# Zero rows of the routed buffers written inside the attention's loop, and Wg turned in other PSUM banks

## The reference

```python
x = x + xattn(layernorm(x), ctx)        # ctx: 32 x 1601 x 512
x = x + attn(layernorm(x))              # "attn": a recurrence over the 64 steps
x = x + ffn(layernorm(x))               # 8 experts, 2 of them per token

# xattn: softmax over the context, feats = [h, hq, h*hq, h*hc] @ W_qv + b_qv
# attn:
z = sigmoid(x @ Wg.T + bg)
h = df * h + (1 - df) * (z_t * (x_t - (h @ Wr.T + br)))     # df = sigmoid(decay)
y = (layernorm(h) * ln_w + ln_b) @ Wo.T + bo
# ffn: top 2 of softmax(x @ gate_w.T), weights normed, then per expert
out = (silu(x @ gate) * (x @ up)) @ down
```

## Time and profile before

| | |
|---|---|
| median of 3 runs | 1304.49 us (1302.57 to 1305.15) |
| the profiled execution | 1303.37 us |
| its span, first to last instruction | 1301.6 us |
| mean granted TensorE clock | 0.969 of full speed |
| PE, DVE, ACT, POOL busy | 1204.4, 724.4, 451.6, 591.9 us |
| moved by DMA | 225.22 MB, mean 173 GB/s |

### The profile page before, as it was taken

The page is one execution under the profiler, slowest core; times in us unless marked ns, Lnnn a source line. Parts: engine busy times, 40 slices in busy tenths (PEclk is TensorE's granted clock), DMA queues, the critical chain, the costliest instruction groups (busy, mean ns, idle before and its releaser), DMA issues. The chain is left out here.

```text
span 1301.6 us, 29765 instructions
## 1 busy us (share of the span) xinstructions
PE 1204.4 (93%) x10484; PEld 742.4 (57%) x10485; DVE 724.4 (56%) x1508; ACT 451.6 (35%) x1006; POOL 591.9 (45%) x641
## 2 busy tenths in 40 slices
PE   2899999999999999999989699997699999999993
PEld 1344444444444344444367477775588888888882
DVE  5555566655557665555379667787632323223235
ACT  3443445443445544344156243543111111212110
POOL 1123333222333321333069567887296564531972
PEclk9899999999999999999989799997799999999997
DMA  9644565444566444466074678752114344412556
GB/s 332 240 166 163 212 218 207 142 170 152 200 218 218 171 158 159 173 212 211 10 235 138 220 246 292 258 185 109 50 58 165 139 161 145 161 56 72 154 162 186
DMA packets 95187, 225.22 MB, mean 173 GB/s; under 512 B 10088, under 2 KB 26600, under 8 KB 91024
## 3 DMA queue, kind: packets, MB, share of 16 engines
q1 hardware_dynamic: 78912, 181.05, 40.3%
q0 software_dynamic: 10288, 33.57, 7.6%
q10 hardware_dynamic: 5920, 9.72, 2.3%
HBM read 178.95 MB, written 45.35 MB: 172 GB/s over the span
## 5 line engine op out<-in xcount | busy, mean ns | idle before, releaser
L323 POOL TENSOR_TENSOR wb<-wb,w 128x512 f32<-128x512 f32 x120 | 149.4, 1277 | 338.3 <-ACT wb L509 338.3
L393 PE MATMUL S<-ctxT,x 32*64 32x416 f32 (+1 forms) x4096 | 184.9, 508 | 13.9 <-DVE ctxT L649 13.3
L393 PEld LDWEIGHTS S<-ctxT,x 32*64 32x64 f32 x4096 | 109.3, 132 | 90.8 <-issue 44.8
L631 DVE STREAM_TRANSPOSE ctxT<-ctx_one 128x1024 f32<-128x1024 f32 (+1 forms) x128 | 115.0, 947 | 24.6 <-DMA ctx_one<-in_ctx_dram 24.5
L428 PE MATMUL O<-ctx_one,probsT 128*64 128x512 f32 (+1 forms) x448 | 110.7, 609 | 0.0
L523 ACT ACTIVATE x<-S,w2R,w3R 128x128 f32<-128x128 f32 x256 | 93.6, 492 | 19.2 <-PE S L384 19.2
L2048 POOL TENSOR_TENSOR w_low<-w_low,w_high 128x2048 fp32r<-128x2048 f32 x21 | 96.8, 4609 | 1.7
L2226 DVE TENSOR_TENSOR f_hL<-f_TH,f_hH 128x512 fp32r<-128x512 f32 x39 | 27.0, 692 | 116.9 <-ACT f_hH L2186 116.9
L2191 ACT ACTIVATE sg<-f_G 128x512 f32<-128x512 f32 x39 | 23.4, 599 | 193.7 <-PE f_G L2133 193.7
L1511 PE MATMUL Pb<-w_high 128*32 128x128 f32 x2016 | 70.7, 283 | 10.3 <-DVE w_high L1802 10.2
L509 ACT ACTIVATE wb<-w,hcb 128x512 f32<-128x512 f32 x120 | 77.6, 746 | 0.0
(11 more groups left out here) (298 smaller groups left out, 2491.5 us busy)
## 6 DMA issues: line engine op xcount, KB each, us to landing
ctx_one<-in_ctx_dram SPq DMA_DIRECT2D x64, 512.0 KB, 4.5
x<-in_ctx_dram SPq DMA_DIRECT2D x16, 1536.0 KB, 9.5
ctx_two<-in_ctx_dram SPq DMA_DIRECT2D x16, 1536.0 KB
ctx_one<-in_ctx_dram SPq DMA_DIRECT2D x64, 256.0 KB, 5.4
w_low<-_L_ffn_gate_up_proj_dram POOLq DMA_DIRECT2D x10, 1024.0 KB, 7.7
f_xt<-routed_x SPq DMA_DIRECT2D x39, 256.0 KB, 2.7
routed_y<-f_yt SPq DMA_DIRECT2D x39, 256.0 KB, 2.0
w_low<-_L_ffn_gate_up_proj_dram SPq DMA_DIRECT2D x6, 1024.0 KB, 12.8
```

Source lines behind the costliest of these rows:

```text
L323: pool.tensor_tensor(wb[:, slot, b], wb[:, slot, b], w0[:, c], ALU.add).then_inc(wb_ready, 1)
L393: last = pe.matmul(S[64 * b:64 * b + 64, a, 0:tiles * Q], qr[a * Q:(a + 1) * Q, k, 64 * b:64 * b + 64], ctxT[a * Q:(a + 1) * Q, 0:tiles, b ...
L631: return dve.transpose(ctxT[:, pos:pos + n, b], src[:, i:i + n, :].rearrange("p t (k r) -> p t k r", r=Q))
```

## The change

Two edits that have nothing to do with each other.

*The zeros.* The buffers `routed_x` and `routed_y` are declared in a new class `RoutedRows` ahead of the attention, which gets it as `rows`. POOL clears a tile `zero` of 128x128 at the attention's start. SP writes 24 tiles of `routed_y`, two at the end of each body of the loop, and behind the last step, ahead of `ahead.load`, the 8 pads and 7 spare tiles of `routed_x`. Each write is 256 KB as before, but its source is the 128x128 tile taken four times, so its runs are 128 floats instead of 512. `routed_y` gets one tile more (24 in place of 23). In the recurrence the writes, their waits and the `memset` go; `load_ahead` keeps the experts' weights.

*Wg.* TensorE turns Wg into the banks `WR` instead of `g_T` and `g_Z`. Its wait for all four `wgL` moves from ahead of `turn(0, 0)` to ahead of `gates(0, 0)`. On DVE `low_x(0, 0)` moves ahead of `statistics(2, 0)`.

```diff
+            def zeros(out):
+                sp.dma_start(out, zero[:, None, :].to_broadcast([P, C, P])).then_inc(zero_out, 16)
...
+            assert rows.UNWRITTEN == 2 * (PAIRS - 4)
             step(0, 0, True, False)
+            sp.wait_ge(zero_set, 1)
             with sp.Fori(0, (PAIRS - 4) // 2) as i:
                 step(2 * i + 1, 1, True, True)
+                zeros(rows.unwritten[sp.snap(4 * i)])
+                zeros(rows.unwritten[sp.snap(4 * i + 1)])
                 step(2 * i + 2, 0, True, True)
+                zeros(rows.unwritten[sp.snap(4 * i + 2)])
+                zeros(rows.unwritten[sp.snap(4 * i + 3)])
             step(PAIRS - 3, 1, True, True)
             step(PAIRS - 2, 0, False, True)
+            for e in range(sh.E):
+                zeros(rows.pads[e])
+            for n in range(rows.spare):
+                zeros(rows.spares[n])
...
+            sp.wait_ge(zero_out, 16 * (rows.UNWRITTEN + sh.E + rows.spare))
...
                 pool.wait_ge(tail_zero, b + 1)
+            pool.memset(zero[:], 0.0).then_inc(zero_set, 1)
             pool.memset(mhalf[:], -0.5).then_inc(consts, 1)
...
-        WT = T + Z
         WR = [stack.enter_context(nc.psum_tensor(f"g_W{n}", [P, 512], F32)) for n in range(C)]
...
             pe.wait_ge(ahead.w_in, 16)
             for k in range(C):
                 for c in range(C):
-                    last = pe.transpose(WT[k][:, c * P:(c + 1) * P], wg_rows[:, k, c * P:(c + 1) * P], ident[:])
+                    last = pe.transpose(WR[k][:, c * P:(c + 1) * P], wg_rows[:, k, c * P:(c + 1) * P], ident[:])
                 last.then_inc(wT_full, 1)
-            pe.wait_ge(wL_ready, C)
...
             turn(0, 0)
             turn(1, 1)
+            pe.wait_ge(wL_ready, C)
             gates(0, 0)
...
-                act.copy(wgH[:, :, k * P:(k + 1) * P], WT[k][:].rearrange("p (c e) -> p c e", c=C)).then_inc(wH_ready, 1)
+                act.copy(wgH[:, :, k * P:(k + 1) * P], WR[k][:].rearrange("p (c e) -> p c e", c=C)).then_inc(wH_ready, 1)
...
-                dve.tensor_tensor(wgL[:, :, part], WT[k][:].rearrange("p (c e) -> p c e", c=C), wgH[:, :, part].bitcast(F32),
+                dve.tensor_tensor(wgL[:, :, part], WR[k][:].rearrange("p (c e) -> p c e", c=C), wgH[:, :, part].bitcast(F32),
...
             for k in range(C):
                 low_w(k)
+            low_x(0, 0)
             statistics(2, 0)
-            low_x(0, 0)
...
+class RoutedRows:
+
+    UNWRITTEN = 24
+
+    def __init__(self, nc, sh):
         self.region = P + sh.N
         self.tiles = (2 * sh.N + sh.E * (P - 1)) // P
         self.spare = self.tiles - 2 * sh.N // P
         self.rows = sh.E * self.region + self.spare * P
+        self.x_rows = nc.dram_tensor("routed_x", (self.rows, sh.D), F32, kind="Internal").ap()
+        self.y_rows = nc.dram_tensor("routed_y", (self.tiles * P, sh.D), F32, kind="Internal").ap()
+        regions = self.x_rows[0:sh.E * self.region, :].rearrange("(e r) d -> e r d", e=sh.E)
+        self.pads = regions[:, 0:P, :].rearrange("e p (s i) -> e p s i", i=P)
+        self.spares = self.x_rows[sh.E * self.region:, :].rearrange("(n p) (s i) -> n p s i", p=P, i=P)
+        last = self.y_rows[(self.tiles - self.UNWRITTEN) * P:, :]
+        self.unwritten = last.rearrange("(n p) (s i) -> n p s i", p=P, i=P)
+        assert self.tiles - self.UNWRITTEN <= sh.N // P
...
-        zero, xn3T = ex.rows(1, 2)[0:2]
+        xn3T = ex.rows(1, 2)[1]
...
-            pads = [e * rt.region for e in range(E)] + [E * rt.region + i * P for i in range(rt.spare)]
-
-
-
-            AHEAD = TILES - 2
-            first_unwritten = sh.N // P
-            unwritten = [range(first_unwritten + i, rt.tiles, AHEAD) for i in range(AHEAD)]
-
             def load_ahead(k):
 
-                if k == 0:
-                    sp.wait_ge(zero_set, 1)
-                else:
+                if 0 < k <= ex.SLOTS * ex.PARTS:
                     sp.wait_ge(h_ready, ST * k)
-                for r in pads[k::AHEAD]:
-                    sp.dma_start(rt.x_rows[r:r + P, :], zero[:]).then_inc(zero_out, 16)
-                for t in unwritten[k]:
-                    sp.dma_start(rt.y_rows[t * P:(t + 1) * P, :], zero[:]).then_inc(zero_out, 16)
-                if 0 < k <= ex.SLOTS * ex.PARTS:
                     ex.load(sp, (k - 1) // ex.PARTS, (k - 1) % ex.PARTS)
...
-            assert ex.SLOTS * ex.PARTS < AHEAD
-            for k in range(AHEAD):
+            assert ex.SLOTS * ex.PARTS < TILES
+            for k in range(TILES):
                 body(k, k % 2)
                 load_ahead(k)
-            for k in range(TILES - 2, TILES):
-                body(k, k % 2)
-            sp.wait_ge(zero_out, 16 * (len(pads) + sum(len(u) for u in unwritten)))
...
-            pool.memset(zero[:], 0.0).then_inc(zero_set, 1)
```

## The result

The changed kernel took **1295.07 us** (median of 4 runs, 1293.51 to 1297.39) beside 1303.67 for the kernel before on the same chip: a ratio of 0.9931, 95% interval 0.9919 to 0.9944, or 9.0 us (7.3 to 10.6) faster. The two intervals do not meet (7.0 against 7.3); the forecast's 6.1 lies inside the second only. So two questions stand: where the microseconds come from, and why the size moves.

The account below looks back on a forecast made before the run. With TensorE busy 93% of the span, only transfers an engine waits for were taken to matter. Recurrence 5.0 plus gates 1.1 gave 6.1 us off, 1298.4 against the median; own range 1296.5 to 1300.5, 8-in-10 range 1295.8 to 1302.8.

Parts of the forecast that it names:

- 1, zeros out of the recurrence: Recurrence: without the zero writes x tiles load in time and POOL's long waits go; 5.0 us off.
- Five at 9.72 would be 48.6: Recurrence: five bodies took 53.53 us against 48.6 at the later bodies' pace; the 4.9 excess was taken as 5.0.
- a short wait absorbed: Recurrence: the body from 791.28 took 9.63 us with a load wait inside, so short waits were held to be absorbed.
- above, the full 9.3: Recurrence: upper bound of the zeros' gain, all 9.3 us of POOL's waits for x tiles.
- 25 points of the 89: Recurrence: 16 zeros fill 13.8 of 55 us of DMA time, so the 0.89 share falls to some 0.65.
- Rival B: Recurrence: x loads on about four engines stay late and only the gates gain; 1303.4 us, chance 0.15.
- 2 and 3, zeros in the attention: Attention: 24 writes in its loop and 15 behind its last context parts fit idle DMA time and cost nothing.
- the forecast 0.86: Attention: each zero write takes 0.86 us, like stores of `u` and `c`; two fill 1.7 us of a body's hole.
- 4, Wg: Gates' start: Wg turned in Wr's banks and the low part sooner start the first gates matmul 1.1 us earlier.
- its bounds of 0.6 and 1.5: Gates' start: gain of 0.6 us if the clock returns to full speed no earlier, 1.5 if it returns earlier by more.
- What is late next: Gates: tile 2's statistics come 1.5 us later harmlessly; POOL follows TensorE and carries the 1.1 us to the stage's end.
- rival A: Gates: TensorE's gain ends before POOL's transfer-bound start, so only the recurrence gains; 1299.5 us, chance 0.14.

Follow-up runs that it names:

- before again: The kernel before, unchanged, run for one more profiled execution: 1304.36 us in its one run.
- e2: The kernel before with only Wg's edit, the zeros still in the recurrence: 1303.31 us, ratio 0.9998 to the kernel before.
- e4: The kernel before with each x tile of the recurrence loaded by four transfers instead of one, all zeros in place: 1297.45 us, ratio 0.9961.
- e5: The changed kernel with the x tile's load in four transfers as well: 1295.87 us, ratio 0.994 to the kernel before.
- e1: The changed kernel with Wg turned in the old banks as before, so only the zeros' edit: 1296.75 us, ratio 0.9953 to the kernel before.
- e8: The changed kernel with six zero writes in each attention body in place of two: 1296.78 us, ratio 0.9951 to the kernel before.
- e9: The changed kernel with the 15 writes of pads and spare tiles back in the recurrence: 1297.55 us, ratio 0.995 to the kernel before.
- e10: The changed kernel with 40 transposes of the identity behind TensorE's last gates matmul: 1296.41 us, ratio 0.9964 to the kernel before.
- the repeat: The changed kernel, unchanged, timed again in more rounds: 1296.14 us (10 runs), ratio 0.9961 to the kernel before.

## Why the prediction was right and where it was wrong

The time came out at 1295.07, 3.3 us under the forecast of 1298.4. Of these, 0.8 are the kernel before: its median was 1304.49 when I wrote and 1303.67 in the result. The rest is in the sum: terms that were too small, the recurrence's first, and 2.0 us in stages put at nothing.

*1, zeros out of the recurrence: right in kind, the term too small.* The step that failed is "Five at 9.72 would be 48.6: the excess is 4.9 us ... I take 5.0". It took one stretch of five bodies for the whole, and one execution for the kernel. On the same execution the scan lost 5.8: 5.0 in the five bodies from 801.52 on and 0.8 ahead of them, where I had called a short wait absorbed on the strength of one body. That reading was wrong too: the only wait in the stretch from 791.28 to 800.91 is the beginning of the one of 2.65, which starts at 799.48. Three waits in before's timeline of POOL, the first two ahead of 800:

```profile
770.83 0.74 POOL L1440 TENSOR_TENSOR w_high<-w_high,bo_b 128x256 f32<-128x256 f32 x1 [1.55 <-DMA w_high<-x]
780.40 0.73 POOL L1440 TENSOR_TENSOR w_high<-w_high,bo_b 128x256 f32<-128x256 f32 x1 [1.53 <-DMA w_high<-x]
833.65 0.74 POOL L1440 TENSOR_TENSOR w_high<-w_high,bo_b 128x256 f32<-128x256 f32 x1 [1.85 <-DMA w_high<-x]
```

The bodies that go with them on DVE took 9.69, 10.03 and 11.44 us; after's took 9.28, 9.66 and 9.63. So a wait of 1.5 us costs 0.4 here, one of 1.85 costs 1.8 and that of 2.65 costs 3.6 (13.28 against 9.69). In before again and e2 waits of 1.5 and 1.6 cost 0.3 and 0.4, of 1.7 some 1.2, of 2.3 and 2.4 early in the scan 1.1 and 1.3, and of 2.8 to 3.0 from 2.4 to 3.7. These two executions lost 7.5 and 8.5 us in all. The bound "above, the full 9.3" was one execution's as well: the sum of the waits was 12.4 and 13.2 in the others.

*The reason given for it was wrong.* "25 points of the 89" predicted a share of some 0.65; it is 0.77, and e4 cured the waits at 0.91. The share is a mean over sixteen engines and does not say which are busy. And what other transfers come sooner when the zeros are gone was not in the sum: by the bytes above, 1.1 of the 4.2 MB, an estimate of 6 of the 13 points between 0.64 and 0.77; no row shows the rest. Rival B named the place, a load on few engines, but its outcome (1303.4) did not come: by its own arithmetic 192 KB take 9.4 us of a body's 9.7, which is just in time, and the longest wait left in after is 1.1. Both the narrow load and the zeros are needed to make x late; taking either away is worth the same within the intervals, 6.1 and 5.1 us, and taking both (e5) shows no more.

*2 and 3, zeros in the attention: right in the cost, not in the place.* Nothing measurable, at 0.73 to 1.15 us a write against the forecast 0.86 (23 stores counted; the 5.76 MB of the earlier trace rows are those of 22, so 0.90). The hole was shortened by 0.75 us and not by about 2, since part of the writes went out in the crowded stretch ahead of it; with six writes a body the length stays too.

*4, Wg: the direction right, the 1.1 in part luck.* The gates end at 70.18 on the mean of the four executions with the old form (before, its repeat, e1, e4) and at 69.14 on that of the seven with the new one (after, its repeat, e2, e5, e8, e9, e10): 1.0 us, close to the forecast. But that mean mixes executions whose clock fell at different times, and the gain hangs on this. Where it fell at Wg's transposes the new form ends at 69.67 and 69.59 (e2, e10) and the old at 69.69 (e4): 0.0 to 0.1. Where these ran at full clock the new form ends at 68.74 to 69.22 (five executions) and the old at 70.77 (before again): 1.8 on the mean, with the first matmul 1.4 sooner (7.03 to 5.67). The forecast read one execution; its bounds of 0.6 and 1.5 allowed for when the clock comes back, but not for when it falls. The end times do not resolve the term: e2 alone says 0.3 us faster, from 1.6 slower to 2.1 faster. "What is late next" held: POOL's first step was released by the decay row's transfer (659.55) and the gain arrived behind it, so rival A did not come.

*The sum.* With the terms from the same pair of executions, 5.8 + 2.0, it would have been 7.8. The other 2.0 of 9.8 are the attention (1.6) and what follows the scan (0.4), put at nothing; no experiment tied either to an edit, and the attention's end varies by more (652.0 to 654.6) with the zeros in it. So that the first timing fell below the range is in part chance. The lower end, 1295.8, was set too near all the same: the loss to late x was taken from one execution, and others lost up to 8.5. The repeat, 5.1, errs the other way. What stays open is the mean loss of the kernel before: its executions timed with e1 and e2 went from 1299.13 to 1307.01 (19), after's in the repeat from 1294.30 to 1298.14 (10), and only three of before's kind were seen in a trace.

## What to carry to other kernels

A transfer that comes late in a crowded stretch has two cures, less traffic and a wider transfer; look first at how many engines it runs on, since the mean DMA share does not tell. Price a wait by the whole chain it sits in (first step to last), over more than one execution: here waits of up to 1.2 us cost next to nothing, of 1.5 a quarter of themselves, and of 1.7 and more from half of themselves to more than themselves. An end time that moves by 2 us from one execution to the next cannot settle a term of 1 us; compare the stage from its own start, over several executions, and only those whose clock fell alike.

## What the hardware showed that I had not expected

The granted clock at the gates' start falls at a different time from execution to execution, of the same kernel too: 1.3 us behind the first Wg transpose in before and 5.7 in its repeat, 5.7 in after, and at the first transpose in e2 and e4. The 16 transposes take 1.94 or 3.52 us by that. At the recurrence's start it was at 0.50 from 726 to 732 in every execution, and 2.2 us of idle in place of 6.5 did not change it. Four transfers of 64 KB went better than one of 256 KB: POOL's 9.3 us of waits for x were gone with the engines fuller than before (0.91 against 0.89).
